# A 1x1 convolution with pyramid pooled attention in fp32: tiles convolved in pairs, half of the input channels by seven products

## What is computed

```python
qk    = relu(bn(conv1x1(x, qk_w)))          # 256 channels
val   = relu(bn(conv1x1(x, v_w)))           # 512 channels
key   = psp(qk)                             # max pooling to 1+9+36+64 = 110 cells
value = psp(val)
scores = softmax(einsum('bnc,bcs->bns', query, key) * 256 ** -0.5)   # query is qk, 4096 pixels
y = einsum('bns,bsc->bnc', scores, value)
y = bn(conv1x1(y, out_w))
return x + y
```

## Time and profile before

| | |
|---|---|
| median of 3 runs | 1411.49 us (1408.1 to 1411.98) |
| profiled execution, its time | 1407.77 us |
| its span, first to last instruction | 1406.0 us |
| PE busy | 1381.3 us, 98% |
| DVE busy | 844.9 us, 60% |
| ACT busy | 488.8 us, 35% |
| POOL busy | 507.3 us, 36% |

### The profile page before, as it was taken

One profiled execution on the slowest core, in us unless ns is written; L12 is line 12 of the kernel. 1 busy time (PEld: TensorE's weight loads), 2 busy tenths in 40 slices (PEclk: granted clock), 3 DMA queues, 4 the chain that ended last, 5 costly groups with the idle time before them and its releaser, 6 DMA issues.

```text
span 1406.0 us, 15809 instructions
## 1 busy us (share of the span) xinstructions
PE 1381.3 (98%) x6029; PEld 1129.6 (80%) x6029; DVE 844.9 (60%) x1760; ACT 488.8 (35%) x688; POOL 507.3 (36%) x226
## 2 busy tenths in 40 slices
PE   7999999999999999999999999999999999999997
PEld 6888888888888888888888888888888887788875
DVE  6434655557556576456665566555765567786666
ACT  4112323423333323333334233333333334673422
POOL 2233323323333324234233333333332342865532
PEclk9999999999999999999999999999999999999999
DMA  5113224434345344345254353453443444788426
GB/s 195 60 60 96 84 98 172 151 130 169 123 147 180 125 145 172 127 150 176 95 179 139 132 178 121 149 180 121 148 165 129 156 166 139 270 294 273 145 90 239
DMA packets 107213, 213.38 MB, mean 152 GB/s; under 512 B 3418, under 2 KB 3458, under 8 KB 107138
## 3 DMA queue, kind: packets, MB, share of 16 engines
q1 hardware_dynamic: 106562, 211.32, 42.9%
q10 hardware_dynamic: 576, 1.05, 0.2%
HBM read 145.25 MB, written 67.11 MB: 151 GB/s over the span
## 4 chain that ended last, share of the span: by engine, by line
PE 95%; DVE 3%; ACT 1%; issue 0%; DMA 0%; SPq 0%; ACTq 0%; DVEq 0%
PE conv_ps L389 25%; PE conv_ps L387 25%; PE conv_ps L388 24%; PE out_ps L431 4%; PE out_ps L432 4%; PE out_ps L433 4%; PE score_ps L402 2%; PE score_ps L403 2%; PE score_ps L404 2%; PE sum_ps L415 1%; PE sum_ps L414 1%; PE sum_ps L442 0%; PE sum_ps L444 0%; PE sum_ps L443 0%; DMA xa<-x 0%
## 5 line engine op out<-in xcount | busy, mean ns | idle before, releaser
L387 PE MATMUL conv_ps<-xh,wh 128*128 128x512 f32 x1536 | 601.8, 392 | 0.0
L389 PE MATMUL conv_ps<-xl,wh 128*128 128x512 f32 x1536 | 601.3, 391 | 0.0
L388 PE MATMUL conv_ps<-xh,wl 128*128 128x512 f32 x1536 | 598.2, 389 | 0.0
L751 DVE TENSOR_REDUCE row_max<-conv_ps 128x64 f32<-128x512 f32 (+2 forms) x576 | 284.0, 530 | 406.1 <-ACT q L579 217.8
L327 POOL TENSOR_TENSOR xl<-xa,xh 128x1024 fp32r<-128x1024 f32 x142 | 341.6, 2410 | 410.5 <-ACT xh L558 410.5
L389 PEld LDWEIGHTS conv_ps<-xl,wh 128*128 128x128 f32 x1536 | 288.5, 188 | 63.6
L388 PEld LDWEIGHTS conv_ps<-xh,wl 128*128 128x128 f32 x1536 | 288.8, 188 | 63.1
L387 PEld LDWEIGHTS conv_ps<-xh,wh 128*128 128x128 f32 x1536 | 288.6, 188 | 61.2
L333 POOL TENSOR_TENSOR q_l<-q,q_h 128x1024 fp32r<-128x1024 f32 x64 | 155.5, 2430 | 443.9 <-ACT q_h L585 443.9
L579 ACT ACTIVATE q<-conv_ps,shift 128x512 f32<-128x512 f32 x128 | 88.1, 689 | 291.2 <-PE conv_ps L389 288.2
L590 ACT ACTIVATE score_ps<-score_ps 128x512 f32<-128x512 f32 x56 | 32.6, 582 | 430.3 <-PE score_ps L404 429.9
(11 more groups left out here) (172 smaller groups left out, 961.6 us busy)
## 6 DMA issues: line engine op xcount, KB each, us to landing
xa<-x SPq DMA_DIRECT2D x73, 1024.0 KB, 7.5
xo<-x SPq DMA_DIRECT2D x58, 1024.0 KB, 5.3
out<-xo SPq DMA_DIRECT2D x57, 1024.0 KB, 4.2
q<-x SPq DMA_DIRECT2D x4, 1024.0 KB, 5.3
out<-q SPq DMA_DIRECT2D x4, 1024.0 KB, 4.2
q<-v_w ACTq DMA_DIRECT2D x4, 256.0 KB, 4.4
xa<-x SPq DMA_DIRECT2D x2, 512.0 KB, 5.5
q<-out_w SPq DMA_DIRECT2D x1, 1024.0 KB, 7.7
```

What stands on the lines that cost most here:

```text
L387: nc.tensor.matmul(bank(s, c)[:, :], wh[:, k, cols], hi, start=(k == 0), stop=False)
L388: nc.tensor.matmul(bank(s, c)[:, :], wl[:, k, cols], hi, start=False, stop=False)
L389: last = nc.tensor.matmul(bank(s, c)[:, :], wh[:, k, cols], lo, start=False, stop=(k == KC - 1))
L751: last = nc.vector.tensor_reduce(row_max[:, c, n, :], src[:, r0_ * W:r1_ * W].rearrange("p (r w) -> p w r", w=W), AX.X, ALU.max)
```

## The change

Steps 0 and 1 stay single tiles, and so do those of the last image. The 54 tiles between them are convolved as 27 pairs (s = 1 to 27, tiles 2s and 2s + 1), and a pair's six channel groups as three pairs of groups, each a product of 2 x 2 blocks for the first half of the input channels. These 2 x 2 blocks are multiplied by Strassen's scheme in Winograd's form: 7 block products for 8. The second half of the input channels is multiplied as before (`plain`). `pair_product` is one such unit: 15 block products of three matmuls in four banks. Between them it runs work of the attention, handed in as `fill1` to `fill3`.

The scheme needs sums. Those of the weights are made once at the start (`combine_weights`, 12 DVE passes, with `combinations_hi` on ACT and `combinations_lo` on DVE). Those of x are made by POOL for each pair (T1, T2, T3 and again T1: `first_sums`, `last_sum`), and a pair is split in 9 parts (`PARTS`), 11 blocks of 512 columns instead of 8. Those of the products are made three ways: by PE adding into a bank; by ACT, which copies u1 to another bank (`copy_u1`) and u5 to SBUF (`copy_u5`); and by DVE, which adds u5 to a bank (`make_u4`, `make_u7`). In a pair A = 2s - 8 and A + 1 get their scores, B0 = A - 1 and A their sums. SBUF space for it comes from smaller rings: `xh` and `xl` hold one pair, `q_h` one tile instead of two, `e_h` two and not six, and the residual and output ring three half tiles.

```diff
-        xa = sb("xa", [P, 2, KC, TN])
-        xo = sb("xo", [P, 2, OC, TN])
+        xa = sb("xa", [P, 2, 2, 2, TN])
+        xo = sb("xo", [P, 3, 2, TN])
+        tt = sb("tt", [P, 2, TN])
+        u5 = sb("u5", [P, TN])
         q = sb("q", [P, NT, QC, TN])
...
+        PARTS = [
+            (xa[:, 0, 0, 0:1, :], 0, 1),
+            (tt[:, 0:1, :], 8, 9),
+            (tt[:, 1:2, :], 9, 10),
+            (xa[:, 0, 0, 1:2, :], 1, 2),
+            (xa[:, 0, 1, 0:1, :], 2, 3),
+            (xa[:, 0, 1, 1:2, :], 3, 4),
+            (xa[:, 1, 1, :, :], 6, 8),
+            (xa[:, 1, 0, :, :], 4, 6),
+            (tt[:, 0:1, :], 10, 11),
+        ]
...
+            B11, B21, B12, B22 = (xa[:, 0, t, k, :] for t in range(2) for k in range(2))
+            T1, T2, T3 = tt[:, 0, :], tt[:, 1, :], B12
+            def first_sums(s):
+                for t in range(2):
+                    wait_x(pool, 2 * s + t)
+                if s > 1:
+                    pool.wait_ge(x_lo, x_parts(s))
+                nc.gpsimd.tensor_tensor(T1, B12, B11, ALU.subtract).then_inc(t_made, 1)
+                pool.wait_ge(t_made, 4 * (s - 1) + 1)
+                nc.gpsimd.tensor_tensor(T2, B22, T1, ALU.subtract).then_inc(t_made, 1)
+                nc.gpsimd.tensor_tensor(T3, B22, B12, ALU.subtract).then_inc(t_made, 1)
+            def last_sum(s):
+                pool.wait_ge(x_lo, x_parts(s) + 2)
+                pool.wait_ge(t_made, 4 * (s - 1) + 3)
+                nc.gpsimd.tensor_tensor(T1, B21, T2, ALU.subtract).then_inc(t_made, 1)
+            def split_parts_lo(s):
+                split_part_lo(s, 0)
+                split_part_lo(s, 1)
+                last_sum(s)
+                for i in range(2, OPS):
+                    split_part_lo(s, i)
             def split_q_lo(a):
                 pool.wait_ge(q_hi, a + 1)
...
+            def pair_product(s, j, fill1, fill2, fill3):
+                n, g, x0 = product(s, j), pair_group(s, j), x_parts(s)
+                u1, u5_bank, u6, u7 = pair_banks(n)
+                m1, m2 = (slice(c * P, (c + 1) * P) for c in HALVES[j])
+                ms = slice(j * P, (j + 1) * P)
+                def times(out, hi, lo, b, start=False, stop=False):
+                    nc.tensor.matmul(out[:, :], hi, xh[:, b, :], start=start, stop=False, skip_group_check=True)
+                    nc.tensor.matmul(out[:, :], lo, xh[:, b, :], start=False, stop=False, skip_group_check=True)
+                    return nc.tensor.matmul(out[:, :], hi, xl[:, b, :], start=False, stop=stop, skip_group_check=True)
+                def plain(out, m, b, stop):
+                    times(out, wh[:, 2, m], wl[:, 2, m], b)
+                    return times(out, wh[:, 3, m], wl[:, 3, m], b + 1, stop=stop)
+                def x_ready(i):
+                    if j == 0:
+                        pe.wait_ge(x_lo, x0 + i)
+                x_ready(1)
+                if s == 1:
+                    pe.wait_ge(s_lo, j + 1)
+                pe.wait_ge(rows_pooled, g - 3)
+                times(u1, wh[:, 0, m1], wl[:, 0, m1], 0, start=True).then_inc(p1_done, 1)
+                fill1()
+                x_ready(2)
+                pe.wait_ge(rows_pooled, g if n == 0 else g - 1)
+                times(u7, sh[:, 0, ms], sl[:, 0, ms], 8, start=True).then_inc(p5_done, 1)
+                x_ready(3)
+                pe.wait_ge(u1_copied, n + 1)
+                times(u6, sh[:, 1, ms], sl[:, 1, ms], 9).then_inc(u2_done, 1)
+                x_ready(4)
+                times(u1, wh[:, 1, m1], wl[:, 1, m1], 1)
+                x_ready(8)
+                plain(u1, m1, 4, stop=True).then_inc(conv_done, 1)
+                fill2()
+                x_ready(5)
+                pe.wait_ge(u4_made, n + 1)
+                times(u6, sh[:, 2, ms], sl[:, 2, ms], 2).then_inc(u3_done, 1)
+                x_ready(6)
+                times(u5_bank, sh[:, 3, ms], sl[:, 3, ms], 3)
+                x_ready(7)
+                plain(u5_bank, m1, 6, stop=True).then_inc(conv_done, 1)
+                fill3()
+                pe.wait_ge(u7_made, n + 1)
+                plain(u7, m2, 6, stop=True).then_inc(conv_done, 1)
+                plain(u6, m2, 4, stop=False).then_inc(x0_used, 1)
+                x_ready(9)
+                times(u6, wh[:, 1, m2], wl[:, 1, m2], 10, stop=True).then_inc(conv_done, 1)
...
+                pair_product(s, 0,
+                             lambda: (projections((A - 2, 2)), sums_of(B0)),
+                             lambda: projections((A - 2, 3)),
+                             lambda: None)
+                projections((B0, 0), (B0, 1))
+                pair_product(s, 1,
+                             lambda: scores_of(A),
+                             lambda: (projections((B0, 2)), turn_values()),
+                             lambda: sums_of(A))
+                pair_product(s, 2,
+                             lambda: projections((B0, 3)),
+                             lambda: projections((A, 0), (A, 1)),
+                             lambda: scores_of(A + 1))
...
+            def split_part_hi(s, i):
+                raw, b0, b1 = PARTS[i]
+                if i in (1, 2, 4, 8):
+                    act.wait_ge(t_made, 4 * (s - 1) + {1: 1, 2: 2, 4: 3, 8: 4}[i])
+                else:
+                    wait_x(act, 2 * s + (1 if i in (5, 6) else 0))
+                if s == 1:
+                    if i not in (1, 2, 8):
+                        act.wait_ge(conv_done, CC if i in (0, 3, 7) else 2 * CC)
+                else:
+                    n, g = product(s - 1, 2), pair_group(s - 1, 2)
+                    used, count = [(p1_done, n), (p5_done, n), (u2_done, n), (conv_done, g), (u3_done, n),
+                                   (conv_done, g + 1), (conv_done, g + 2), (x0_used, n), (conv_done, g + 3)][i]
+                    act.wait_ge(used, count + 1)
+                nc.scalar.activation(xh[:, b0:b1, :], raw, ACT.Copy).then_inc(x_hi, 1)
+            def copy_u1(s, j):
+                n = product(s, j)
+                u1, _, u6, _ = pair_banks(n)
+                act.wait_ge(p1_done, n + 1)
+                act.wait_ge(rows_pooled, pair_group(s, j) - 2)
+                nc.scalar.activation(u6[:, :], u1[:, :], ACT.Copy).then_inc(u1_copied, 1)
+            def copy_u5(s, j):
+                n = product(s, j)
+                act.wait_ge(p5_done, n + 1)
+                wait(act, u7_made, n)
+                nc.scalar.activation(u5[:, :], pair_banks(n)[3][:, :], ACT.Copy).then_inc(u5_copied, 1)
+            def weights_hi(i):
+                j = W_ORDER[i]
+                act.wait_ge(w_turned, i + 1)
+                src = setup_ps[i % 4][:, :].rearrange("p (k n) -> p k n", k=KC)
                 dst = wh[:, :, j * P:(j + 1) * P] if j < CC else woT_h[:, :, (j - CC) * P:(j - CC + 1) * P]
...
+            def make_u4(s, j):
+                n = product(s, j)
+                _, u5_bank, u6, _ = pair_banks(n)
+                dve.wait_ge(u5_copied, n + 1)
+                dve.wait_ge(u2_done, n + 1)
+                dve.wait_ge(rows_pooled, pair_group(s, j))
+                nc.vector.tensor_tensor(u5_bank[:, :], u6[:, :], u5[:, :], ALU.add).then_inc(u4_made, 1)
+            def make_u7(s, j):
+                n = product(s, j)
+                _, _, u6, u7 = pair_banks(n)
+                dve.wait_ge(u3_done, n + 1)
+                nc.vector.tensor_tensor(u7[:, :], u6[:, :], u5[:, :], ALU.add).then_inc(u7_made, 1)
...
+                    pool_tile_cells(1, 0, CC)
+                else:
+                    pool_cells((t0 - 2) % NT, VC, CC, pair_group(s, 0))
+                    pool_cells((t0 - 1) % NT, VC, CC, pair_group(s, 0))
+                if batch_ended:
+                    finish_grids(VC, CC)
                     finish_keys()
-                pool_rows(s, 0)
-                if last_of_batch:
+                make_u4(s, 0)
+                if B0 >= 0:
+                    refine(B0)
+                    normalise(B0)
+                pool_pair_rows(s, 0, 0)
+                make_u7(s, 0)
+                if A >= 2:
+                    add_out(A - 2, 2)
+                    add_out(A - 2, 3)
+                if B0 >= 0:
+                    split_p_lo(B0)
+                if batch_ended:
+                    finish_grids(0, VC)
                     finish_values(0, VC)
-                pool_rows(s, 1)
-                pool_rows(s, 2)
-                if ap >= 0:
-                    add_out(ap, 0)
-                    add_out(ap, 1)
-                pool_rows(s, 3)
-                if s == 0:
-                    for j in range(CC, PAR):
-                        scale_weights(j)
-                    spread_shift()
-                if ac >= 0:
-                    split_e_lo(ac)
-                pool_rows(s, 4)
-                if ap >= 0:
-                    add_out(ap, 2)
-                    add_out(ap, 3)
-                if last_of_batch:
-                    make_values(ac // NT)
```

(43 more changed lines are left out.)

## The result

The kernel got slower: 1465.43 us as a median of 4 runs (1461.24 to 1467.62) against 1409.8 (1407.34 to 1411.98) for the kernel before on the same chip, a ratio of 1.0392 (95% interval 1.0357 to 1.0426). The forecast was 1437 and its range ended at 1460. The direction was right, and the loss a little more than twice as large as forecast. The profiled execution took 1467.33 us with a span of 1465.6, 59.6 more than the span before.

The account below looks back on a forecast made before the run. PE, with work for 98% of the span, was taken as the bound. Waits of 80.9 us against 55.6 saved gave +25.3 on 1411.5, so 1437 us; range 1390 to 1460, the forecast's own 1420 to 1447.

Parts of the forecast that it names:

- 243 matmuls: On PE, 45 matmuls for 48 in each of 81 units, 0.229 us each: 55.6 us saved.
- parts 6 and 7, 18 ordinary pairs: PE waits for the next pair's x split through ACT and POOL: 0.9 us a pair, 16.2 us (0 to 27).
- five ends of images: Pairs s = 8, 12, 16, 20, 24: PE waits for keys, u7, values and parts, 7.5 us each, 37.5 together.
- first four pairs: Pairs s = 1 to 4, the first ones without fills: waits of 6.2, 3.6, 3.6 and 9.8, together 23.2 us (18 to 30).
- setup: DVE, already the bound there, gets 12 sums of weights and three low parts: 4 us (2 to 7).
- last image: Change from pairs to the last image: two more DVE sums, six more PE matmuls to hide them: 0 (-2 to 2).
- The price of `make_u4`: At image ends keys precede `make_u4` on DVE, their sums held up by POOL's passes: PE waits 3.8 us.
- the case of 3.4: At image ends, the third sum for the keys gets in before POOL's `split_q_lo(A)`: PE waits 3.4 us, not 4.2.
- `make_u7` was priced at 0.7: At image ends, DVE's five passes from `make_u4` take 3.4 us against 12 matmuls, 2.75: 0.7 us with the restart.
- `values_lo` was priced at 1.9: At image ends, `values_lo` stands behind ten DVE steps and PE wants it at 8.2: wait 1.2 to 2.2, taken as 1.9.
- a rival of 0.12: Clock falls where PE idles at image ends, six places at 2 to 3 us: 1452 us; chance 0.12, longer DVE queue included.
- covered rival: Waits mostly covered, no wait for parts 6 and 7, keys free of POOL: 37 us lost, 1393 us; chance 0.20.

Follow-up runs that it names:

- run apart: Kernel before with 243 of its matmuls left out (part of the low by high product) and nothing else changed: 1353.74 us, ratio 0.961.
- the last run: Changed kernel with keys and values moved, part 6 split between stores, weights turned later, POOL's first sums held until the values' low parts: 1399.23 us, ratio 0.9931.

## Why the prediction was right in kind and short by half

| term, us | forecast | measured |
|---|---|---|
| 243 matmuls | -55.6 | -55.7, run apart |
| parts 6 and 7, 18 ordinary pairs | 16.2 | 15.8 |
| five ends of images | 37.5 | 35.9 |
| first four pairs | 23.2 | 22.4 |
| setup | 4 | 6.6 |
| last image | 0 | -0.5 |
| matmuls at the lower clock | none | 19.0 |
| remainder | none | 16.0 |

Each measured wait is the distance of two starts less m, with the 0.1 of the restart. Setup and last image are differences of times between the two profiled executions. The last line is what is left of the 59.6 between the two spans: 59.6 + 55.6 - 80.2 - 19.0 = 16.0, with 80.2 the sum of the five lines of waits, forecast at 80.9. That the two agree so closely is in part luck, since some of the terms came out right for another reason than the forecast had.

**The saving** was right: m is 0.229, and PE never short of work.

**Ordinary pairs.** Forecast 0.9, measured 0.77 and 0.11 of restart. The chain is the one named, with ACT's parts 6 and 7 from 394.27 and POOL's from 395.40:

```profile
395.40 4.74 POOL L442 TENSOR_TENSOR xl<-xa,xh 128x1024 fp32r<-128x1024 f32 x2 [2.42 <-ACT xh L817]
...
400.19 0.50 PE L563 MATMUL conv_ps<-xh,wh 128*128 128x512 f32 x1 [0.61 <-POOL xl L442]
```

**Ends of images.** 0.88, 3.91 and 2.39 make 7.2 a pair against 7.5. The price of `make_u4` (3.9) came out, by POOL's three passes as forecast. That it did so to 0.01 is luck: 3.8 was the middle of 4.2 and 3.4, the third sum (L1208) got in ahead of `split_q_lo(A)`, which was the case of 3.4, and a scaling (L1212) then stood behind that pass and brought the wait to 3.78. `make_u7` was priced at 0.7 and made PE wait for nothing, because the matmuls ahead of it came at 0.43; where they came at 0.23, in the run in which POOL holds its pass, PE waited 0.32 to 0.35 for it. `values_lo` was priced at 1.9 and took 2.39:

```profile
384.84 1.54 DVE L1275 TENSOR_TENSOR vo_l<-vo,vo_h 128x512 fp32r<-128x512 f32 x1
...
384.55 1.28 POOL L442 TENSOR_TENSOR xl<-tt,xh 128x512 fp32r<-128x512 f32 x1
...
386.48 0.47 PE L653 MATMUL out_ps<-e_h,vo_h 128*128 128x512 f32 x1 [2.16 <-issue]
```

The view names issue as the releaser of L653, but `vo_l` ended at 386.38 and PE started 0.1 later; taking `values_lo` forward removed the wait, which shows it.

**First pairs** 6.1, 2.9, 3.0 and 10.5, against 6.2, 3.6, 3.6 and 9.8. In the first the forecast had the chain through POOL alone, and its total is right by luck: PE waited 2.80 for POOL, 1.79 for the copy of u1 and 1.21 for row maxima, and the rest is restarts. The fourth has one wait of 0.62 for the copy of u1 that the forecast lacked.

**Setup.** The first matmul of tile 1 behind the turned weights starts at 40.13 and did at 33.48: 6.6 for 4. The three low parts of the combined weights stand on DVE between row maxima, one of them 2.28 us long. **The last image**, from the first matmul of tile 56 to the end, took 232.9 us against 233.4 for the same matmuls.

**The failed step** is that the sum left the clock out and made it a rival of 0.12 ("Six such places at 2 to 3 us each"). The argument against it was one wait of 2.61 us after which matmuls came at 0.23, and the waits that the same prediction had at those places were of 3.8. The row nearer to them was the earlier trace rows, where PE had run 1.46 of 4 us and the clock fell. Measured: 62 matmuls at 0.43 behind the six waits for `make_u4` (12.3 us at 0.427 less m), 18 behind three of the six for the values, and most of the rest behind waits of the setup and of the first pair; the kernel before had 12 in all. So the rival happened, at 19.0 us for its 15. With it the sum would have given 1456, so the clock alone doesn't fill the gap: the sum also had nothing for gaps too short to count as waits.

**The remainder** of 16.0 us has parts that the trace shows. The distance of matmuls with no wait between them is 0.2296 us, and 0.22875 before, which is 4.6 us over 5427 of them. Most of that is in the projections (0.2326 against 0.2287) and in the matmul right behind one (0.2314 against 0.2262); between block products it is 0.2286 against 0.2284. The projections have 18 gaps of 0.15 and 22 restarts of 0.11, together 5.2 us (before, 4 such restarts). Some 6.5 us are spread over other places, the first start behind a wait at the lower clock (0.56 and not 0.34, ten times) among them. Why the even distance grew stays open.

A small slip in the prediction changes nothing: the 2.9 us a pair of its covered rival are 0.7 + 0.1 + 1.9 = 2.7 by its own terms.

## What to carry to other kernels

A wait of PE has two prices: its length, and the matmuls behind it at half the clock. For a wait of 3.8 to 4.7 us the second was 7 to 13 matmuls here, up to 2.6 us; put it into the sum, not beside it. A wait that comes from small DVE passes beside POOL's can be mended where it is made: hold POOL back if it stands still afterwards anyway. One such line gave 19.5 us, another 8.4. Reordering DVE gave as much when keys and values were both moved (21.3), and 5.4 when only the keys were. Of the 55.6 us that the matmuls were worth, 9.6 were kept, and only with all the moves of the last run together.

## What was not expected of the hardware

- The clock fell behind three of five equal waits of 2.31 us. After the wait that ended at 386.48 the matmuls came at 0.23; after the one that ended at 563.70, the next start came 0.56 later and six more at 0.43. The same code gives images of 176.1 and 178.9 us.

```profile
561.20:563.70 2.50, 0.34 (x2) 0.03 (x1) 2.50 (x4) 1.50 (x3) 2.42 (x3) 0.97 0.25 93
563.70:567.70 4.00, 4.00 (x11) 3.19 (x12) 0.65 (x2) 0.08 (x1) 3.50 (x3) 0.59 0.69 204
```

- A cast of 220 columns took 1.33 us beside a POOL pass and 0.28 without one, and a scaling of 110 columns 2.09 and 0.28. The passes with two inputs in SBUF were known from the earlier trace rows; these have one input in SBUF besides a scalar at most.
- Twelve matmuls of no use at each end of an image made the changed kernel 9.8 us faster.
